# Router logits moved from slot 4 to slot 6, the steps behind them to the next period, and gate scores stored apart from rows

## The chip, the cores and the metric

The kernel runs on one core of one Trainium2 chip. The metric is the device time of the whole program in microseconds, the median of several runs. The profiler records one more execution; its own time stands beside the median below. PE is TensorE, DVE VectorE, ACT ScalarE, POOL GpSimd and SP SyncE; the last is used here to issue DMAs.

## What is computed

The reference is one transformer layer over 8 sequences of 384 tokens of width 512: 256 tokens that a state-space kernel makes from `x`, and 128 of `txt`. Grouped-query attention with rotary embedding follows, then a mixture of 64 experts (top 6 of each token, 64 places for each expert) beside a shared expert. What the change touches is the router:

```python
h = jnp.concatenate([_L0_tok_ref(x, ...), txt], axis=1)
h = h + _L0_attn_ref(_layernorm(h), Wq, Wk, Wv, Wo)
h = h + _L0_ffn_ref(_layernorm(h), gate_w, ...)
# in _L0_ffn_ref
logits = x @ gate_w.T
scores = jax.nn.softmax(logits, axis=-1)
topk_w, topk_i = jax.lax.top_k(scores, K)
...
pos = jnp.zeros((TK,), jnp.int32).at[order].set(pos_sorted)   # place within the expert
valid = pos < CAP
```

## The kernel before

The program has three phases: the state-space kernel (to about 135 us), attention with routing and the first two sequences of the shared expert (to about 924 us), and the experts (to the end). The change lies in the second, `attention_phase`.

**Periods and slots.** Every engine has a queue of its own, whose order is written out by hand. All of them run `for b in ITERATIONS` (b from -1 to 7), and in it 16 slots `n`, one for each of the 16 attention heads. I call an iteration with number b period b. A steady period takes about 78.7 us; period 1 runs from about 271 us, period 3 from 428 us, period 6 from 663 us, period 7 from 737 us. Five sequences are in work at once: a = b+1 is normalised, projected and turned (slots 0 to 7), and its raw scores and row maxima are made (slots 8 to 15); b has its attention (`scores`, `exponentials`, `values`); c = b-1 has its output projection (slots 9 to 15); d = b-2 is routed; e = b-3 has its table entries scattered. The flags `nxt`, `prev2` and `prev3` say whether a, d and e exist. The last period, 7, has no a.

**The routing steps of sequence d, before.** PE turns the normalised rows in slots 2 and 3 (`turn_x2`, L978) and makes the logits in slot 4 (`logits`, L985) in PSUM bank 7. ACT copies them to `at_lg` (L1145). DVE takes maxima and their indices (`routing` step 4, L1405 to L1411), the one-hot tables and `at_mask` (step 5, slot 5, L1414 to L1423). ACT makes the exponentials of the gate (L1152, slot 5). PE makes the places from the mask with a triangular matrix (`places`, L996, slot 6, bank 7). DVE scales the gate scores into columns 512 to 575 of the row buffer (step 6, slot 6, L1426 to L1428) and makes positions from places (L1434 to L1436, slot 6; `at_lg` is used again as `over`). POOL adds the first place of each expert and multiplies with the one-hot table (`places` on POOL, L1597 to L1603, slot 7). One period later DVE sums to slot numbers (`slots`, L1441 to L1445, slot 1), and POOL scatters them with 18 indirect DMAs (L1616, from slot 8). SP stores rows and scores together (`store_rows`, L781).

**Beside it, for sequence a.** `project_q` and `project_kv` (L874) on PE in slots 1 to 5, `rope` on DVE (L1338 to L1340) one slot behind each, the sum of its two halves on POOL (`rope_sum`, L1588, slots 3, 4 and 6), the copy of v on ACT (L1209, slots 3, 4 and 6), and in slot 7 `turn_heads` (L953) on PE, with ACT's copies (`qhi` L1230, bf16 L1129 and L1133) and DVE's remainders (`q_lo`, L1346). From slot 8 on each raw score (`raw`, L916) waits for the row maximum (`row_maximum`, L1355) of the one two before it, since two PSUM banks are used in turn, and the first waits for the last `q_lo`. DVE's `statistics(a + 1)` (L1305) in slot 4 waits for the rows of the next sequence from DRAM. POOL also makes `out_lo` (L1592, slots 0, 1 and 5), released by ACT's `out_hi` (L1186).

## Time and profile before

| | us |
|---|---|
| median of 3 runs (lowest to highest) | 1470.17 (1469.13 to 1474.4) |
| the profiled execution, its own time | 1472.85 |
| its span, first to last instruction | 1471.1 |
| busy: PE, DVE, ACT, POOL | 1248.9, 757.1, 419.8, 498.9 |
| mean granted TensorE clock | 0.943 |

The page's busy numbers are sums over three phases with different limits; the timelines of single engines tell where in a period an engine stands and who released it. In a timeline row stand the start, the duration of a merged group, engine and line, what it writes and reads, and in brackets the idle time before it with the work that ended that idle time. An entry "x8" is a group of 8 instructions.

### The profile page before, as it was taken

How to read it: one execution, taken by the hardware profiler on the slowest of the kernel's cores; microseconds unless marked ns; L12 is line 12 of the kernel's file. 1: busy time of each engine (PE TensorE's matmuls, PEld its weight loads, DVE VectorE, ACT ScalarE, POOL GpSimd, SP SyncE). 2: the span in 40 equal slices, each digit the busy share in tenths (PEclk: the TensorE clock that was granted, in tenths of full speed). 3: DMA queues.
4: the chain of work that ended last, by engine and by line, in shares of the span. 5: the costliest groups of instructions: out<-in, count | busy, mean ns of one | idle time of the engine just before them, and what ended most of it. 6: DMA issues, size and time to landing. Idle time of an engine off the chain costs nothing. (4 is left out here: it accounts for less than half of the span.)

```text
span 1471.1 us, 23499 instructions
## 1 busy us (share of the span) xinstructions
PE 1248.9 (85%) x9192; PEld 795.6 (54%) x9192; DVE 757.1 (51%) x1667; ACT 419.8 (29%) x695; POOL 498.9 (34%) x453
## 2 busy tenths in 40 slices
PE   5263778889898999999987879999999999969995
PEld 5252443445454454646444868666666666646662
DVE  7993566666776867786854352232233222312321
ACT  2221214444444443535354421111111111111110
POOL 0000101111213434343466374334444434343444
PEclk9597779999999999999999899999999999989998
DMA  3033231312425151524271484799999999888993
GB/s 113 1 75 85 53 72 42 84 42 71 122 60 133 36 136 22 151 42 127 45 230 43 133 277 61 221 312 298 309 327 343 302 329 349 264 259 298 332 284 41
DMA packets 141109, 239.82 MB, mean 163 GB/s; under 512 B 61368, under 2 KB 81480, under 8 KB 141000
## 3 DMA queue, kind: packets, MB, share of 16 engines
q1 hardware_dynamic: 117160, 214.10, 45.8%
q0 software_dynamic: 23840, 24.23, 9.2%
q8 instruction: 73, 1.20, 0.3%
q14 instruction: 36, 0.29, 0.1%
HBM read 175.59 MB, written 38.90 MB: 146 GB/s over the span
## 5 line engine op out<-in xcount | busy, mean ns | idle before, releaser
L1993 POOL DMA_INDIRECT out_rows<-mo_y,mo_scatter_half x128 | 180.9, 1413 | 253.9 <-DMA out_rows<-mo_y,mo_scatter_half 183.7
L1355 DVE TENSOR_REDUCE at_maxes<-at_ps 128x1 f32<-128x384 f32 x384 | 195.3, 552 | 63.3 <-PE at_ps L916 56.6
L1122 ACT ACTIVATE bulk<-at_ps 128x1152 f32<-128x1152 f32 x128 | 144.6, 1129 | 272.2 <-PE at_ps L883 250.5
L1616 POOL DMA_INDIRECT slot_table<-at_toki,at_si x144 | 143.6, 997 | 105.7 <-DVE at_maxes L1355 74.0
L70 PE MATMUL mo_ps<-arena_view,arena_view 128*117 128x384 f32 (+1 forms) x864 | 168.8, 344 | 1.1 <-PEq L570 1.1
L70 PEld LDWEIGHTS mo_ps<-arena_view,arena_view 128*117 128x117 f32 (+1 forms) x864 | 146.5, 179 | 14.6 <-issue 14.5
L916 PE MATMUL at_ps<-late_view,late_view 128*128 128x384 bf16 x384 | 117.0, 355 | 35.9 <-DVE at_maxes L1355 18.1
L874 PE MATMUL at_ps<-arena_view,arena_view 128*128 128x512 f32 (+1 forms) x576 | 115.6, 352 | 3.8 <-ACT arena_view L1209 2.3
L874 PEld LDWEIGHTS at_ps<-arena_view,arena_view 128*128 128x128 f32 x576 | 90.7, 193 | 36.9 <-issue 22.4
L916 PEld LDWEIGHTS at_ps<-late_view,late_view 128*128 128x128 bf16 x384 | 31.2, 98 | 145.4 <-DVE at_maxes L1355 108.5
L883 PE MATMUL at_ps<-arena_view 97*128 97x384 f32 x384 | 97.8, 364 | 9.6 <-DMA arena_view<-at_mrow 5.1
L1968 DVE SCALAR_TENSOR_TENSOR mo_hm<-mo_sil,mo_wcol,mo_ps 128x352 f32<-128x352 f32 x32 | 18.6, 581 | 157.2 <-ACT mo_sil L1892 140.6
L874 PE MATMUL at_ps<-late_view,late_view 128*128 128x512 f32 x288 | 92.9, 438 | 6.2 <-DVE at_hr L1388 3.4
L1588 POOL TENSOR_TENSOR arena_view<-arena_view,arena_view 128x640 f32<-128x640 f32 x24 | 37.3, 1556 | 173.5 <-DVE arena_view L1340 173.4
L1592 POOL TENSOR_TENSOR late_view<-arena_view,late_view 128x384 fp32r<-128x384 f32 x32 | 32.2, 1016 | 178.4 <-ACT late_view L1186 178.3
L1838 PE MATMUL mo_ps<-late_view,mo_xgT 128*64 128x352 f32 x512 | 80.6, 468 | 12.5 <-DVE mo_xgT L1961 12.5
L902 PE MATMUL at_ps<-bulk,at_ones 128*32 128x384 f32 x768 | 87.9, 528 | 1.8 <-issue 1.4
L78 PE MATMUL mo_ps<-arena_view,arena_view 117*128 117x512 f32 (+1 forms) x324 | 78.9, 397 | 4.8 <-DVE arena_view L1925 4.8
L883 PEld LDWEIGHTS at_ps<-arena_view 97*128 97x128 f32 x384 | 68.5, 195 | 26.2 <-ACT bulk L1122 8.3
L902 PE MATMUL at_ps<-bulk,arena_view 128*32 128x384 f32 x768 | 82.6, 504 | 0.0
L1838 PE MATMUL mo_ps<-bulk,mo_xgT 128*64 128x352 f32 x512 | 79.3, 462 | 0.2 <-DVE mo_xgT L1961 0.2
L78 PEld LDWEIGHTS mo_ps<-arena_view,arena_view 117*128 117x128 f32 (+1 forms) x324 | 59.6, 188 | 20.9 <-ACT arena_view L1880 5.5
...
## 6 DMA issues: line engine op xcount, KB each, us to landing
...
```

The source lines that it names most:

```text
L70: m = T.matmul(out, self.gu[:, wa, g, k, self.SO[c]:self.SO[c] + self.SW[c]], self.x2[:, xa, k, :], start=(n == 0), stop=(n == last))
L78: m = T.matmul(out, self.h[0:self.SW[c], xa, c, s * P:(s + 1) * P], self.d[0:self.SW[c], wa, c, :], start=(n == 0), stop=(n == last))
L874: m = T.matmul(out, xs[:, xa, k, x_cols], ws[:, wa, k, w_cols], start=(n == 0), stop=(n == 3 * KC - 1))
L883: m = T.matmul(ps[:, kt, 0:SEQ], QT[:, NH + h // REP, kt * P:(kt + 1) * P], QT[:, h, :], start=True, stop=True)
L902: m = T.matmul(ps[HD * j:HD * (j + 1), 3 + sums, 0:SEQ], w, PT[:, (REP * G + j) % RING, kt, :], start=(kt == 0), stop=(kt == NT - 1))
L916: T.matmul(ps[:, raw_bank(a, u), 0:SEQ], qb[:, r, s * P:(s + 1) * P], kb[:, g, :], start=True, stop=True).then_inc(raw_scores, 1)
L1122: A.activation(PT[:, N % RING, :, :], ps[:, 0:NT, 0:SEQ], ACT.Exp, scale=float(HD) ** -0.5)\
L1355: V.tensor_reduce(maxes[:, half, s, h:h + 1], ps[:, raw_bank(a, u), 0:SEQ], AX.X, ALU.max, negate=True)\
L1588: G.tensor_tensor(r1[:, s], r1[:, s], r2[:, s % 2], ALU.add).then_inc(rope_add, 1)
L1616: G.indirect_dma_start(slot_table, bass.IndirectOffsetOnAxis(ap=si[:, e % 2, m:m + 1], axis=0), toki[:, e % 2, m // TOPK:m // TOPK + 1], N ...
L1838: m = M.matmul(ps[CAP * e:CAP * (e + 1), 1 + g, 0:I], xgT[:, k, CAP * e:CAP * (e + 1)], wgu[j][:, e, g, k, :], start=(k == 0), stop=(k == ...
L1993: G.indirect_dma_start(acc_halves, bass.IndirectOffsetOnAxis(ap=scatter_half[:, half, 2 * p + e:2 * p + e + 1], axis=0), y[:, p % 2, e, co ...
```

## The change

The logits move from slot 4 to slot 6 (in periods with a next sequence), and everything behind them goes to the next period, so that a sequence is routed as e and not as d: maxima and indices (step 4) to slot 1, one-hot tables and mask (step 5) to slot 2, exponentials to slot 2 on ACT, PE's places to slot 4, gate scores (step 6) to slot 3, positions (now step 7 of its own) to slot 4, POOL's places to slot 5, `slots` on DVE to slot 7 (it was slot 1). The scatter stays in slots 8 to 15 of the same period. In period 7 the sequence e is finished in slots 0 to 5 and d is routed in slots 4 to 9 as before; the scatters of e start at slot 4 and not 2. Rows are stored as soon as they are normalised, the gate scores by a DMA of their own (`store_scores`), 384 pieces of 64 words for each sequence, with a semaphore `scores_stored` that DVE's step 6, SP and POOL wait for. Who waits for bank 7 changes with it: `turn_heads` and `project_out` wait for the logits' copy and not for the positions.

```diff
+        ROUTE_SLOT = {2: (5,), 3: (6,), 4: (7,)}
+        LAST_ROUTE_SLOT = {0: (4, 5), 1: (6,), 3: (7,)}
...
             def store_rows(d):
+                sp.wait_ge(x2_ready, NT * (d + 1))
+                sp.dma_start(xrow[d * SEQ:(d + 1) * SEQ, 0:D].rearrange("(s p) d -> p s d", p=P),
+                             x2_of(d)[:, :, 0:D]).then_inc(x2_stored, 16)
+
+            def store_scores(d):
                 sp.wait_ge(score_rows, d + 1)
-                sp.dma_start(xrow[d * SEQ:(d + 1) * SEQ, :].rearrange("(s p) d -> p s d", p=P), x2_of(d))\
-                    .then_inc(x2_stored, 16)
+                sp.dma_start(xrow[d * SEQ:(d + 1) * SEQ, D:D + E].rearrange("(s p) d -> p s d", p=P),
+                             x2_of(d)[:, :, D:D + E]).then_inc(scores_stored, 16)
...
                 if i == 2:
-                    wait(pe, pos_read, a - 2)
+                    wait(pe, lg_copied, a - 2)
...
                     for q in steps[0:1]:
                         values(G, q)
-                    if prev2 and n == 4:
+                    if prev3 and n == (4 if nxt else 2):
+                        places(e)
+                    if prev2 and n == (6 if nxt else 4):
                         logits(d)
-                    if prev2 and n == 6:
+                    if prev2 and not nxt and n == 6:
                         places(d)
...
-                    if prev2 and n == 5:
+                    if prev3 and n == (2 if nxt else 1):
+                        gate_exponentials(e)
+                    if prev2 and not nxt and n == 5:
                         gate_exponentials(d)
...
                     dve.wait_ge(gexp_ready, NT * (d + 1))
+                    wait(dve, scores_stored, 16 * d)
...
-                if n == 6:
+                if n == 7:
                     dve.wait_ge(pos_ready, d + 1)
...
-                    if prev3 and n == 1:
-                        slots(e)
+                    if prev3 and nxt and n == 1:
+                        routing(e, 4)
...
-                    if prev2:
-                        routing(d, n)
+                    if prev3:
+                        for step in (ROUTE_SLOT if nxt else LAST_ROUTE_SLOT).get(n, ()):
+                            routing(e, step)
+                    if prev3 and n == (7 if nxt else 4):
+                        slots(e)
...
-                    if prev2 and n == 7:
+                    if prev3 and n == (5 if nxt else 3):
+                        places(e)
+                    if prev2 and not nxt and n == 7:
                         places(d)
...
-                    if b == B - 1 and 2 <= n < 8:
-                        scatter(e, 3 * (n - 2), 3 * (n - 1))
+                    if b == B - 1 and 4 <= n < 10:
+                        scatter(e, 3 * (n - 4), 3 * (n - 3))
```

Three places in the engines' queues, first of the kernel before, then of the changed one. Line numbers of the changed kernel are up to 43 higher.

**POOL, slots 3 to 7 of a steady period.** The first row holds the rope sums of slots 3 and 4, the next two the inverse deviation, the fourth `out_lo`; `at_slot`, `at_lg` and `at_hv` mark the places. Before:

```order
L1588 TENSOR_TENSOR arena_view_1739<-arena_view_1739,arena_view_1740 128x640 x2
L1581 TENSOR_TENSOR at_rstd<-at_ve,at_mhalf 128x3
L1583 TENSOR_TENSOR at_shift<-at_shift,at_rstd 128x3
L1592 TENSOR_TENSOR late_view_1738<-arena_view_1748,late_view_1738 128x384
L1588 TENSOR_TENSOR arena_view_1739<-arena_view_1739,arena_view_1740 128x640
L1597 TENSOR_TENSOR late_view_1750<-late_view_1750,at_slot 128x192
L1599 TENSOR_TENSOR late_view_1750<-late_view_1750,at_lg 128x192
L1603 TENSOR_TENSOR at_hv<-at_hot,late_view_1750 128x384 x3
```

and in the changed kernel:

```order
L1631 TENSOR_TENSOR arena_view_1739<-arena_view_1739,arena_view_1740 128x640 x2
L1624 TENSOR_TENSOR at_rstd<-at_ve,at_mhalf 128x3
L1626 TENSOR_TENSOR at_shift<-at_shift,at_rstd 128x3
L1635 TENSOR_TENSOR late_view_1738<-arena_view_1748,late_view_1738 128x384
L1640 TENSOR_TENSOR late_view_1750<-late_view_1750,at_slot 128x192
L1642 TENSOR_TENSOR late_view_1750<-late_view_1750,at_lg 128x192
L1646 TENSOR_TENSOR at_hv<-at_hot,late_view_1750 128x384 x3
L1631 TENSOR_TENSOR arena_view_1739<-arena_view_1739,arena_view_1740 128x640
```

The three rows of places stood behind the last rope sum (slot 6) and now stand ahead of it, behind `out_lo`.

**DVE, from the end of slot 6 to the start of slot 8.** The transposes and the reciprocal are of the softmax sums, the group of five is `q_lo`, `at_maxes` are the row maxima of slot 8. Before:

```order
L1372 STREAM_TRANSPOSE arena_view_1747<-at_ps 128x384
L1373 RECIPROCAL at_rcol<-arena_view_1747 128x12
L1374 STREAM_TRANSPOSE arena_view_1747<-at_rcol 128x384
L1346 TENSOR_TENSOR arena_view_1742<-at_ps,arena_view_1741 128x384 x5
L1355 TENSOR_REDUCE at_maxes<-at_ps 128x1 x2
```

and in the changed kernel:

```order
L1405 STREAM_TRANSPOSE arena_view_1747<-at_ps 128x384
L1406 RECIPROCAL at_rcol<-arena_view_1747 128x12
L1407 STREAM_TRANSPOSE arena_view_1747<-at_rcol 128x384
L1379 TENSOR_TENSOR arena_view_1742<-at_ps,arena_view_1741 128x384 x5
L1476 TENSOR_REDUCE at_sf<-at_hv 128x18
L1478 CAST at_si<-at_sf 128x18
L1479 CAST at_toki<-at_tokf 128x3
L1480 TENSOR_SCALAR at_tokf<-at_tokf 128x3
L1388 TENSOR_REDUCE at_maxes<-at_ps 128x1 x2
```

The four rows of `slots` (`at_sf`, `at_si`, `at_toki`, `at_tokf`) stood in slot 1 and now stand between the last `q_lo` and the first row maximum.

**PE, slot 4 to the start of slot 7.** `gwT` marks the logits, `at_upper` the places, 128x512 and 128x256 are the projections of q and kv, `bulk` the values, 128x384 of `arena_view` alone the scores of a head; the last row is the first turn of the heads. Before:

```order
L985 MATMUL at_ps<-gwT,at_x2T 128x64 x12
L902 MATMUL at_ps<-bulk,at_ones 32x384 x4
L874 MATMUL at_ps<-arena_view_65,arena_view_1737 128x512 x12
L883 MATMUL at_ps<-arena_view_1746 128x384 x3
L902 MATMUL at_ps<-bulk,at_ones 32x384 x4
L902 MATMUL at_ps<-bulk,arena_view_1745 32x384 x4
L874 MATMUL at_ps<-arena_view_65,arena_view_1737 128x256 x12
L883 MATMUL at_ps<-arena_view_1746 128x384 x3
L902 MATMUL at_ps<-bulk,arena_view_1745 32x384 x4
L996 MATMUL at_ps<-at_mask,at_upper 128x64 x9
L883 MATMUL at_ps<-arena_view_1746 128x384 x3
L953 MATMUL at_ps<-late_view_54,arena_view_1739 128x128 x9
```

and in the changed kernel:

```order
L1025 MATMUL at_ps<-at_mask,at_upper 128x64 x9
L922 MATMUL at_ps<-bulk,at_ones 32x384 x4
L894 MATMUL at_ps<-arena_view_65,arena_view_1737 128x512 x12
L903 MATMUL at_ps<-arena_view_1746 128x384 x3
L922 MATMUL at_ps<-bulk,at_ones 32x384 x4
L922 MATMUL at_ps<-bulk,arena_view_1745 32x384 x4
L894 MATMUL at_ps<-arena_view_65,arena_view_1737 128x256 x12
L903 MATMUL at_ps<-arena_view_1746 128x384 x3
L922 MATMUL at_ps<-bulk,arena_view_1745 32x384 x4
L1008 MATMUL at_ps<-gwT,at_x2T 128x64 x12
L903 MATMUL at_ps<-arena_view_1746 128x384 x3
L973 MATMUL at_ps<-late_view_54,arena_view_1739 128x128 x9
```

Logits and places have changed their positions; PE's work up to the turn of the heads is the same.

## Rows read from the trace of the kernel before

**Rows 1.** Page, part 1: busy us (share of the span) of each engine
```profile
PE 1248.9 (85%) x9192; PEld 795.6 (54%) x9192; DVE 757.1 (51%) x1667; ACT 419.8 (29%) x695; POOL 498.9 (34%) x453
```

**Rows 2.** PE's waits, 190 to 860 us: total us, times, longest
```profile
PE at_ps L916 <- DVE at_maxes L1355: 15.2, 28, 1.6
...
PE at_ps L996 <- DVE at_mask L1423: 7.5, 6, 3.1
```

**Rows 3.** PE timeline, period 3, slots 4 to 8: start, us, group [idle <-releaser]
```profile
446.87 2.89 PE L985 MATMUL at_ps<-gwT,at_x2T 128*128 128x64 f32 x24
...
459.26 0.43 PE L996 MATMUL at_ps<-at_mask,at_upper 128*128 128x64 bf16 x9 [0.90 <-DVE at_mask L1423]
459.54 0.77 PE L883 MATMUL at_ps<-arena_view 97*128 97x384 f32 x3
461.45 0.84 PE L953 MATMUL at_ps<-late_view,arena_view 128*128 128x128 f32 x6 [1.15 <-POOL arena_view L1588]
...
467.47 0.80 PE L916 MATMUL at_ps<-late_view,late_view 128*128 128x384 bf16 x2 [0.99 <-issue]
...
469.64 0.82 PE L916 MATMUL at_ps<-late_view,late_view 128*128 128x384 bf16 x2
```

**Rows 4.** PE timeline, period 1, slots 7 and 8
```profile
302.39 0.79 PE L883 MATMUL at_ps<-arena_view 97*128 97x384 f32 x3 [0.50 <-ACT bulk L1122]
...
309.74 0.49 PE L916 MATMUL at_ps<-late_view,late_view 128*128 128x384 bf16 x2 [2.70 <-issue]
```

**Rows 5.** POOL timeline, period 3, slots 4 to 7
```profile
452.93 1.56 POOL L1588 TENSOR_TENSOR arena_view<-arena_view,arena_view 128x640 f32<-128x640 f32 x1 [11.64 <-DVE arena_view L1340]
...
455.73 1.03 POOL L1592 TENSOR_TENSOR late_view<-arena_view,late_view 128x384 fp32r<-128x384 f32 x1
459.81 1.54 POOL L1588 TENSOR_TENSOR arena_view<-arena_view,arena_view 128x640 f32<-128x640 f32 x1 [3.06 <-DVE arena_view L1340]
462.56 0.59 POOL L1597 TENSOR_TENSOR late_view<-late_view,at_slot 128x192 f32<-128x192 f32 x1 [1.21 <-DVE at_lg L1435]
...
463.91 2.68 POOL L1603 TENSOR_TENSOR at_hv<-at_hot,late_view 128x384 f32<-128x384 bf16 x3
```

**Rows 6.** POOL timeline, period 6, slots 5 and 6
```profile
690.79 1.02 POOL L1592 TENSOR_TENSOR late_view<-arena_view,late_view 128x384 fp32r<-128x384 f32 x1 [8.14 <-ACT late_view L1186]
693.92 1.55 POOL L1588 TENSOR_TENSOR arena_view<-arena_view,arena_view 128x640 f32<-128x640 f32 x1 [2.11 <-DVE arena_view L1340]
```

**Rows 7.** DVE timeline, period 3, slots 1 to 8
```profile
433.45 1.34 DVE L1441 TENSOR_REDUCE at_sf<-at_hv 128x18 f32<-128x1152 f32 x1
434.83 0.93 DVE L1443 CAST at_si<-at_sf 128x18 uint32<-128x18 f32 x1
...
436.27 0.69 DVE L1338 TENSOR_TENSOR arena_view<-at_ps,at_cos 128x512 f32<-128x512 f32 x1 [0.24 <-DVE at_tokf L1445]
...
449.82 1.88 DVE L1305 BATCH_NORM_STATS2 at_bn<-arena_view 128x6 f32<-128x512 f32 x3 [5.71 <-DMA arena_view<-in_txt]
...
467.98 1.02 DVE L1355 TENSOR_REDUCE at_maxes<-at_ps 128x1 f32<-128x384 f32 x2 [0.62 <-PE at_ps L916]
```

**Rows 8.** DVE timeline, period 7, slot 9
```profile
776.88 0.25 DVE L1443 CAST at_si<-at_sf 128x18 uint32<-128x18 f32 x1
```

**Rows 9.** ACT timeline, period 3, slot 5
```profile
455.55 0.34 ACT L1152 ACTIVATE late_view<-at_lg,at_nm 128x64 f32<-128x64 f32 x1
```

**Rows 10.** PE timeline, period 3, slot 3
```profile
443.64 1.66 PE L874 MATMUL at_ps<-arena_view,arena_view 128*128 128x256 f32 x12 [0.15 <-ACT arena_view L1209]
```

**Rows 11.** PE timeline, period 6, slot 8
```profile
701.58 0.49 PE L916 MATMUL at_ps<-late_view,late_view 128*128 128x384 bf16 x2 [0.99 <-issue]
...
702.78 0.58 PE L916 MATMUL at_ps<-late_view,late_view 128*128 128x384 bf16 x2
```

**Rows 12.** Busy time by 1 us stretches; the third number from the end is PEclk
```profile
468.00:469.00 1.00, 1.00 (x9) 0.20 (x8) 1.00 (x3) 0.12 (x1) 0.00 (x0) 0.50 0.53 109
```

**Rows 13.** PE timeline, period 7, slot 2
```profile
745.23 0.55 PE L978 MATMUL at_ps<-late_view,late_view 128*128 128x128 f32 x3 [2.26 <-ACT late_view L1163]
```

40 lines of the change are left out of this document (34 added, 6 removed).

## The prediction

> **What bounds the kernel now.** I read the page's busy shares first: PE is busy 85% of the span, DVE 51%, POOL 34%, ACT 29% [rows 1], so a change outside PE pays only where PE waits. Then PE's waits over the attention phase: raw scores wait for the row maxima in slots 8 to 15 (15.2 us in 28 waits), which the change doesn't remove, and the places wait for the mask (7.5 us in 6 waits) [rows 2]. The biggest of those six, 3.1 us, lies after the last period, where the order stays. Last, the timelines of a steady period, to see what comes behind each wait.
>
> In period 3, PE waits 0.90 us for the mask in slot 6 and 1.15 us for the last rope sum before the heads are turned; from the scores of head 7 (459.54) to the first raw score (467.47) it takes 7.93 us [rows 3]. Period 1 has no routing at all: the same stretch, 302.39 to 309.74, still takes 7.35 us [rows 4]. So the floor under slot 7 isn't routing: it is exponentials, `qhi`, bf16 copies and `q_lo` in ACT's and DVE's queues. Of all that routing costs there, only 7.93 - 7.35 = 0.58 us and the 0.90 us of the mask can come back, 1.48 us a period, whatever waits vanish from the list.
>
> **What the change does in periods 2 to 6.** PE's work up to the turn of the heads is the same: 2.89 us of logits go behind the projections, and the places (0.43 us) come ahead [rows 3].
>
> (1) Period 2 routes its d and has no e, so it only loses steps: no mask, no positions, no `slots`. It becomes a period 1 with logits in slot 6. Gain 0.90 + 0.58 = 1.48 us, and some 0.2 us for the places that it no longer makes: **-1.7**.
>
> (2) ACT now makes three gate exponentials of 0.34 us [rows 9], about 1.1 us with their short reads, in slot 2, ahead of the exponentials of head 3 and the copy of v. PE waits for this copy already (0.15 us [rows 10]), so it stands in a chain without slack: the projection of k and v in slot 3 starts about 0.9 us later in periods 3 to 6. Alone this would cut the gain to 0.6 us.
>
> (3) POOL decides the turn of the heads. In slot 5 it makes `out_lo` (1.03 us from 455.73) and then nothing until the last rope sum at 459.81 [rows 5]. The changed queue puts the places between these two. They take 0.59 + 0.59 + 2.68 us and two gaps of 0.08, from 462.56 to 463.91 + 2.68 = 466.59: 4.03 us [rows 5]. They can't start sooner: the rope sum of slot 4 starts at 452.93, released by DVE's rope behind the statistics, which wait 5.71 us for DRAM until 449.82 [rows 5, 7], and this DMA is issued early in the period by SP, in the old order. POOL is then occupied without a break: `out_lo` to 456.76, places to about 460.85, rope sum to about 462.4. Before it ended at 461.35. PE arrives at 459.54 - 0.90 + 0.9 + 0.77, about 460.4, and waits until 462.5, against 461.45 before [rows 3]: instead of a gain of 0.6 a loss of 1.05 us. In period 6, without statistics, ACT releases `out_lo` at 690.79; with PE 2.89 - 0.43 - 0.9 = 1.5 us ahead in slot 5 (logits gone, places come, (2) against it) it starts near 689.4, places end near 694.5, and the rope sum starts there and not at 693.92 [rows 6]: +0.6. Periods 4 and 5 lie between +0.25 and +0.5 by the same sum, for their `out_lo` starts earlier on POOL than in period 3. Together **+2.4**. Bounds: 0.58 saved in each period if POOL had no queue (-2.3), and 4.03 less the idle 3.06 us ahead of the rope sum [rows 5] plus 0.6 for contention, +1.6 in each (+6.4). I take the value of the timeline, since each of its pieces has a row. The wait for `at_lg` (it holds POOL's operand) delays ACT's copy of the logits to the same 461, ahead of the turn; it decides nothing.
>
> (4) `slots` leaves slot 1, where DVE waited 0.24 us before the next rope in any case (433.45 to 436.03, then 436.27 [rows 7]); PE doesn't wait there, and steps 4 to 6 fit into slots 1 to 3 ahead of the 5.71 us wait. I cost that at nothing. In slot 7 it stands where nothing covers it: between the last `q_lo`, which releases the first raw score, and the first row maximum, which releases the third. It is 1.34 us of sum, a cast and small ones. The cast takes 0.93 us in slot 1 beside `out_lo` on POOL and 0.25 us in period 7 [rows 7, 8]; in slot 7 POOL is free, so 1.9 us in all and 0.2 us to the next instruction. A maximum is 0.5 us (two in 1.02 [rows 7]). The third raw score can start 2.6 us after the first. Before it started 469.64 - 467.47 = 2.17 us after it in period 3 [rows 3] and 702.78 - 701.58 = 1.20 us in period 6 [rows 11]. The difference between these two is the clock: in period 3 the granted clock is 0.50 there, which is 1.2 GHz [rows 12], and the first pair of raw scores takes 0.80 us against 0.49 [rows 3, 11]. So the new wait is 0.45 us in the slow periods (3 and 4) and 1.4 us in the others (5 and 6). In the slow ones I add 0.35 us, for the next three raw scores find the maxima late as well. **+4.4** in four periods. Bounds: +1.8 (0.45 each) and +8.4 (the whole 2.1 us).
>
> The Trainium skill ("SBUF — State Buffer", section "SBUF: two separate sides") says that DVE and GpSimd share a port pair as an exclusive lock, held for a whole instruction. The two casts agree with it. If the lock met `slots` in slot 7 too, the term would be 0.7 us larger in each period, by the rows' 0.93 and 0.25.
>
> (5) Period 7 gets steps 4 and 5 of e on DVE and its exponentials ahead of `normalised2(d)` on ACT. PE waits already 2.26 us for that normalisation [rows 13]; 1.1 us more stand ahead of it, and the places of e in slot 2 wait for the mask about as long: +1.35. Against it, POOL's places of d in slot 7 have 9 scatters ahead of them and no longer 18, and DVE waited for them in slot 9: -0.35. **+1.0**, bounds 0 and +3.
>
> (6) Stores: SP issues one more DMA for each sequence. In steady periods rows and scores leave between the loads of the period and the stack of slot 7, where SP's queue waits anyway; behind the last period the wait for the scores stands where the wait for rows and scores stood. POOL's scatters start from slot 8 as before. Nothing.
>
> **Sum.** -1.7 + 2.4 + 4.4 + 1.0 = +6.1 us. Against the profiled execution's own 1472.85 that is 1478.95. It stood 2.7 us above the median of the three runs, so I forecast 1470.17 + 6.1 = **1476.3 us**, 0.4% slower. The experts phase hangs on the end of this one, so all of it counts.
>
> **The rivals.**
> - *The waits go and nothing takes their place.* PE gains the whole 1.48 us in five periods: 1470.2 - 7.4 = 1462.8. For it speaks that both named waits vanish. Against it stand POOL's queue and the maxima. It decides from the point at which POOL's places end before the rope sum's operands are there, and DVE's `slots` meets a PE that waits anyway. On the other side of no change than my forecast: 12%.
> - *Only `slots` costs.* POOL gets to the places sooner than I have it (`out_lo` first of all), and the last rope sum isn't held: -1.7 - 4 x 0.6 + 4.4 + 1.0 = +1.3, 1471.5. For it speaks that in period 6 the margin is only 0.6 us: 20%.
> - *The clock falls further.* The idle time of PE is gathered into two gaps of 2 us around the turn of the heads instead of five of about 1 us. Rows show the granted clock at 0.50 after such a stretch in period 3 [rows 12] and not in period 6. If periods 5 and 6 fall too and 3 and 4 stay low longer, 1.2 us each (0.31 us for each pair of raw scores [rows 3, 11], about four such groups with the values between them): 1476.3 + 4.8 = 1481: 20%.
> - *My forecast*, 1472 to 1480: 48%.
>
> **How the numbers follow.** A measurement of this kernel can tell about 0.5% (7.4 us) from no change: below 1462.8 faster, above 1477.5 slower. The first rival is half below the line: faster 0.07. The clock case and about a third of my own lie above: slower 0.36. The rest is 0.57. The range of 8 in 10 leaves out most of the first rival and the outer half of the clock case: 1465 to 1484.
>
> **What would show it.** In the changed kernel's periods 3 to 5: the mask wait of PE gone; POOL's three places rows straight behind `out_lo` and the rope sum straight behind them with no idle time; PE's turn of the heads waiting some 2 us for L1631; `slots` between `q_lo` and the first maximum; the third raw score 2.6 us after the first; a wait of about 1 us in slot 3 for the copy of v. Periods 3 to 6 should be longer by 1.4 to 2 us, period 2 shorter by 1.7. I am wrong if the turn of the heads comes earlier in the period than before, or if the periods are as long as before although the rows stand so.

## The result

The changed kernel takes 1487.24 us (median of 4 runs, 1484.58 to 1491.80) beside 1472.29 us for the kernel before (4 runs, 1469.13 to 1475.32): a ratio of 1.0117, 95% interval 1.0079 to 1.0155 (the two medians alone differ by 15.0 us, 1.0%). I had forecast 1476.3 with a range to 1484: slower, as forecast, but by more than twice as much, and outside the range. Run again on another chip (e5 below) the changed kernel stood at 1.0094 (1.0053 to 1.0134), 13.8 us by that run's median of before, 1467.92. The times of one kernel on one chip differ by more than the change does (12 executions of the changed kernel in e5: 1470.96 to 1493.42), so I compare stretches of traces below, and ratios within one chip.

The profiled execution took 1484.58 us (span 1482.8). Part 1 of its page, answering [rows 1], says little: nearly the same shares, as many instructions, 8 us more PE time.

```profile
PE 1256.8 (85%) x9192; PEld 801.3 (54%) x9192; DVE 751.3 (51%) x1667; ACT 417.9 (28%) x695; POOL 503.5 (34%) x453
```

PE's waits between 190 and 870 us (total, times, longest), answering [rows 2]:

```profile
PE at_ps L936 <- DVE at_maxes L1388: 19.5, 34, 1.6
PE at_ps L936 <- issue: 18.0, 7, 2.7
PE at_ps L1025 <- DVE at_mask L1456: 7.0, 3, 3.6
...
PE at_ps L894 <- ACT arena_view L1240: 5.6, 8, 0.9
PE at_ps L973 <- issue: 5.3, 4, 1.7
...
PE at_ps L922 <- DVE arena_view L1405: 4.2, 1, 4.2
```

The mask's six waits have become three, in period 7 and behind it. In their place stand 34 waits for maxima where there were 28, the copy of v (0.9 us), the turn of the heads and, once, 4.2 us for L1405 (the inverted sums), a wait that the kernel before doesn't have. The timeline of PE in period 3, slots 3 to 8, answering [rows 3] and [rows 10]:

```profile
446.32 1.67 PE L894 MATMUL at_ps<-arena_view,arena_view 128*128 128x256 f32 x12 [0.92 <-ACT arena_view L1240]
...
458.53 2.89 PE L1008 MATMUL at_ps<-gwT,at_x2T 128*128 128x64 f32 x24
...
463.61 2.14 PE L973 MATMUL at_ps<-late_view,arena_view 128*128 128x128 f32 x9 [1.62 <-issue]
...
470.24 0.61 PE L936 MATMUL at_ps<-late_view,late_view 128*128 128x384 bf16 x2 [1.72 <-issue]
...
472.71 0.97 PE L936 MATMUL at_ps<-late_view,late_view 128*128 128x384 bf16 x2 [0.42 <-DVE at_maxes L1388]
```

The logits are in slot 6 (458.53), no places and no mask stand there; the projection in slot 3 waits 0.92 us; the turn of the heads (L973) waits 1.62; the third raw score starts 2.47 us behind the first. POOL and DVE in the same period, answering [rows 5] and [rows 7]:

```profile
457.03 1.02 POOL L1635 TENSOR_TENSOR late_view<-arena_view,late_view 128x384 fp32r<-128x384 f32 x1
458.01 0.59 POOL L1640 TENSOR_TENSOR late_view<-late_view,at_slot 128x192 f32<-128x192 f32 x1
458.68 0.59 POOL L1642 TENSOR_TENSOR late_view<-late_view,at_lg 128x192 f32<-128x192 f32 x1
459.35 2.67 POOL L1646 TENSOR_TENSOR at_hv<-at_hot,late_view 128x384 f32<-128x384 bf16 x3
461.98 1.53 POOL L1631 TENSOR_TENSOR arena_view<-arena_view,arena_view 128x640 f32<-128x640 f32 x1
```

```profile
469.11 1.02 DVE L1379 TENSOR_TENSOR arena_view<-at_ps,arena_view 128x384 fp32r<-128x384 f32 x2 [0.37 <-ACT arena_view L1261]
470.05 1.34 DVE L1476 TENSOR_REDUCE at_sf<-at_hv 128x18 f32<-128x1152 f32 x1
...
472.09 1.02 DVE L1388 TENSOR_REDUCE at_maxes<-at_ps 128x1 f32<-128x384 f32 x2 [0.21 <-DVE at_tokf L1480]
```

POOL runs through from `out_lo` over the places to the rope sum, which ends at 463.5, where PE starts; DVE makes `slots` (470.05 to 471.9) between the last `q_lo` and the first maximum. Step for step it stands as the prediction drew it, but for `out_lo`, which starts 0.7 us earlier in the period (29.2 us behind the first turn of x, not 29.9). What it had not drawn is in the clock. Busy time of PE in stretches of 4 us around the first raw scores of period 4 (the last numbers are the granted clock, the DMA share and GB/s), first of the kernel before, then of the changed one, starting 3.2 to 3.4 us ahead of the first of them:

```profile
542.98:546.98 4.00, 3.19 (x15) 0.50 0.17 63
546.98:550.98 4.00, 4.00 (x24) 0.74 0.82 167
550.98:554.98 4.00, 3.89 (x28) 1.00 0.81 173
```

```profile
547.46:551.46 4.00, 1.28 (x10) 1.00 0.00 0
551.46:555.46 4.00, 2.80 (x18) 0.62 0.83 172
555.46:559.46 4.00, 4.00 (x20) 0.53 0.87 178
559.46:563.46 4.00, 4.00 (x27) 1.00 0.09 20
```

Before, the clock is at 0.50 (1.2 GHz, the lower of its two levels) while PE turns heads and waits for ACT and DVE in any case, and is back at 1.00 some 2.7 us behind the first raw score (546.37). Now PE idles for 2.7 us ahead of the first raw score (1.28 of 4 us busy, clock 1.00), and the clock falls behind that, for some 6 us, over raw scores and values that bound the period.

### The profile page after: what moved, and what is told of

It reads as the page before. It is cut to its first block and busy times, and to the rows that moved or that the text cites. A ratio compares the mean times of both kernels' runs of the same rounds, so it can differ in the third digit from the quotient of the medians.

```text
span 1482.8 us, 23520 instructions
## 1 busy us (share of the span) xinstructions
PE 1256.8 (85%) x9192; PEld 801.3 (54%) x9192; DVE 751.3 (51%) x1667; ACT 417.9 (28%) x695; POOL 503.5 (34%) x453
## 5 line engine op out<-in xcount | busy, mean ns | idle before, releaser
L2039 POOL DMA_INDIRECT out_rows<-mo_y,mo_scatter_half x128 | 185.3, 1447 | 241.8 <-DMA out_rows<-mo_y,mo_scatter_half 155.0
L936 PE MATMUL at_ps<-late_view,late_view 128*128 128x384 bf16 x384 | 120.7, 367 | 47.2 <-DVE at_maxes L1388 21.8
L903 PE MATMUL at_ps<-arena_view 97*128 97x384 f32 x384 | 100.9, 373 | 11.6 <-ACT bulk L1153 6.5
```

Source lines behind the costliest of these rows:

```text
L903: m = T.matmul(ps[:, kt, 0:SEQ], QT[:, NH + h // REP, kt * P:(kt + 1) * P], QT[:, h, :], start=True, stop=True)
L936: T.matmul(ps[:, raw_bank(a, u), 0:SEQ], qb[:, r, s * P:(s + 1) * P], kb[:, g, :], start=True, stop=True).then_inc(raw_scores, 1)
L2039: G.indirect_dma_start(acc_halves, bass.IndirectOffsetOnAxis(ap=scatter_half[:, half, 2 * p + e:2 * p + e + 1], axis=0), y[:, p % 2, e, co ...
```

## Where the time is

I cut each trace at three kinds of rows: the first turn of x of each period (L946, L926 before), the first turn of x2 in period 7, and the places of sequence 6 behind the last period. All in us; "remote" is the idle time of ACT and DVE that the profile puts down to a cause of that name, over the whole run. It is in all kernels of three of the five sessions and in none of the other two, so it isn't a kernel's own; where it is present the last stretch can't be compared. The profiled execution of e7, 1491.37 us, is the longest of its ten; its excess lies in the last stretch and behind it.

```
kernel                         P2     P3     P4     P5   P6 to   x2 of 7    remote
                                                         x2 of 7 to places
before                        78.84  78.70  78.74  77.62  84.30   90.66      28.7
changed                       76.98  81.22  81.03  80.27  89.28   93.27      44.4
e5 changed, again             77.09  79.12  79.86  80.40  89.31   93.19      13.9
e2 store first                77.77  79.86  80.34  81.86  89.57   86.89       0
e1 slots ahead                77.73  79.67  80.19  78.31  88.24   88.09       0
e3 pool behind                77.07  81.63  81.72  81.99  90.68   89.06       0
e4 before + dummy slots       77.34  79.71  78.58  78.86  85.48   84.06       0
e6 slots ahead, store first   77.70  79.70  80.23  80.07  87.39  102.17      47.3
e7 changed + fillers          76.77  79.03  79.05  79.05  87.62  102.92      40.8
e8 before + fillers           77.71  77.39  77.41  77.45  83.97   91.37      18.4
e9 slots ahead + fillers      76.74  78.24  78.32  78.17  86.79   89.11       0
e10 and pool behind + fillers 76.70  79.67  79.44  78.03  87.00   88.32       0
e11 period 7                  77.70  79.87  80.29  80.17  88.64   83.74       0
e12 all                       76.08  80.70  78.74  78.79  85.54   82.37       0
e13 mid                       76.41  76.74  75.83  75.78  85.15   89.35      46.8
e14 mid, exponentials early   76.13  76.60  76.60  76.60  85.92   86.39      12.0
e15 mid, no filler            77.04  78.33  77.04  77.61  87.45   87.73      12.5
e16 mid, pool ahead           76.78  78.98  78.21  77.74  86.13   84.91      12.7
```

The changed order of periods 2 to 6 was traced four times (changed, e5, e2 and e11, whose edits lie in period 7). The means of the first three against the one trace of before: period 2 -1.6, periods 3 to 5 +6.3 (241.3 against 235.1), period 6 to the turn of x2 +5.1. For the last stretch I take kernels without "remote": e1, e3, e9 and e10 have the changed end, 88.6 on average, e4 that of before, 84.06: +4.6. Sum +14.4 us (14.0 with e11), against 13.8 by the ratio of e5.

This sum is put together from several traces, and it is softer than its digits. In the first pair of traces the last stretch is only 2.6 us longer (93.27 against 90.66), both with "remote", and periods 2 to 7 together 13.2. The changed trace is also 3.8 us late at the start of period 2, ahead of the change, and takes 5.3 us less behind the places of sequence 6 (629.9 against 635.2), a part in which all the traces here lie between 620.8 and 642.3 us. So a time of a single execution says nothing on the change. e3, e4, e9, e10, e14 and e16 were executed once each (1479.40, 1468.54, 1472.40, 1472.38, 1469.11 and 1450.86 us): of these only the stretches can be used. And one trace of before is a narrow base. Period 2 of e4 is the kernel before without any edit, and it took 77.34 us where before has 78.84. In both PE idles 1.15 us ahead of the turn of the heads and 1.00 ahead of the first raw score; behind that score the clock was at 0.57 in before and at 1.00 in e4. The 4 us from it on, before and then e4:

```profile
388.61:392.61 4.00, 4.00 (x21) 0.57 0.72 147
```

```profile
390.02:394.02 4.00, 3.94 (x27) 1.00 0.71 147
```

## The experiments

**e1: slots ahead of q_lo.**

```diff
+                    if prev3 and nxt and n == 7:
+                        slots(e)
                     if nxt and n == 7:
                         for i in range(NTILE):
                             q_lo(a, i)
...
-                    if prev3 and n == (7 if nxt else 4):
+                    if prev3 and not nxt and n == 4:
```

> The changed kernel with one move: slots(e) of the steady periods stands ahead of the five q_lo of slot 7 on VectorE and no longer between them and the first row maxima. There VectorE is idle (5.1 us of waiting for ScalarE in period 4). Length of a period is taken from one turn of x to the next: 81.22, 81.03 and 80.27 us for periods 3 to 5 in the changed kernel, 78.70, 78.75 and 77.62 in the kernel before. If slots costs its own delay alone (the wait of 1.20 us ahead of the third raw score), the periods shorten by 1.2 us each, the granted clock staying at 0.50 over slot 8. If slots is the whole loss, its gap also being what brings the clock down over slot 8, they shorten by 2.3 to 2.6 us each, to 78.5 to 78.9. If it is POOL's queue that costs, by less than 0.5 us.

Ratio to before 1.0012 (0.9975 to 1.0050), against 1.0094 to 1.0117 with `slots` where the change has it. The wait ahead of the third raw score is gone: the first and the third in period 3 of e1,

```profile
468.02 0.78 PE L936 MATMUL at_ps<-late_view,late_view 128*128 128x384 bf16 x2 [1.81 <-issue]
...
470.17 0.82 PE L936 MATMUL at_ps<-late_view,late_view 128*128 128x384 bf16 x2
```

2.15 us apart at half clock, as before. Periods 3 to 5 sum to 238.2, 3.1 less than the mean of the changed order, with a spread from 78.3 to 80.2: in period 5, the short one, the clock is back at 1.00 before the first raw score, in the other two it is at 0.50 behind it. The ratio would make `slots` most of the loss, but with period 6 the stretches give back 4.3 us and no more, and e6, with this edit and another, stands at 1.0049 on another chip. The periods are about 1 us shorter each: between "POOL's queue" and the lower of the two figures that I had set for `slots`, and something else varies.

**e2: the store ahead of the loads.**

```diff
+                if prev3 and not nxt:
+                    store_scores(e)
                 if b == B - 1:
                     load_shared_weights()
-                if prev3 and not nxt:
-                    store_scores(e)
```

> The changed kernel with one move: in period 7 SyncE issues the store of the scores of e ahead of the loads of the shared weights and no longer behind them. In the changed kernel VectorE waits 5.02 us for this store at 775.5 to 780.6, ahead of the scores of d, and TensorE 4.24 us behind it for the inverted sums (783.32). If this store is the loss of period 7, both waits vanish and the tail starts 3.5 to 4.5 us earlier against the start of period 7. If the wait only stands in the place of the 3.4 us that the kernel before waits there for its residual, that one returns and less than 1 us is won. A third way: SyncE now waits for the score rows (ready at 760) before it issues the weights, so that ScalarE's pieces of the weights come 5 us later and the wait turns up there.

Ratio 1.0062 (1.0024 to 1.0100). In the changed kernel DVE stood still in period 7 ahead of the scores of d, since it may not overwrite those of e before they are stored, and `divide`'s inverted sums stand behind it. DVE and PE there:

```profile
780.56 0.18 DVE L1460 RECIPROCAL at_rsum<-at_ssum 128x3 f32<-128x3 f32 x1 [5.02 <-DMA rows_scores<-late_view]
...
782.59 0.58 DVE L1405 STREAM_TRANSPOSE arena_view<-at_ps 128x384 f32<-128x384 f32 x1 [0.22 <-issue]
```

```profile
783.32 1.51 PE L922 MATMUL at_ps<-bulk,at_ones 128*32 128x384 f32 x8 [4.24 <-DVE arena_view L1405]
```

SP issued that store at 768.11, behind the loads of the shared weights (766.59 and 767.02); its 96 KB landed 12 us later. In e2 it is issued at 762.03 ahead of them, neither wait is there, the two stores of this size land 3.4 and 7.8 us after their issue, and no wait for the weights shows. The last stretch takes 86.89 us and not 88.6 (88.1 to 89.1 in four traces), so by this one trace the wait was worth about 1.7 us of its 4.2: the rest is covered by PE's next waits (3.72 us for a residual, 5.53 for `out_lo`).

**e3: POOL's places behind the rope sum.**

```diff
-                    if prev3 and n == (5 if nxt else 3):
+                    if prev3 and not nxt and n == 3:
                         places(e)
...
                         rope_sum(a, KV_SLOT[n - 1])
+                    if prev3 and nxt and n == 6:
+                        places(e)
```

> The changed kernel with one move: GpSimd makes the places of e behind the last rope sum of slot 6 and no longer ahead of it. In period 3 out_lo ends at 458.0, so the sum would run at 458.0 to 459.6 and TensorE, which has its scores done at 461.99, would turn the heads 1.5 us earlier, at about 462.1 instead of 463.61 (33.4 us behind the turn of x; 33.2 in the kernel before). If POOL's queue costs what I forecast, periods 3 to 5 shorten by about 1.5 us each, those of period 3 most. If the time between turn and first raw score is bound elsewhere, the turn comes earlier and the period keeps its length to 0.5 us, the slow stretch of the clock then lying otherwise. Slots has its operand by 463.6 and is not delayed.

Counted from the first turn of x of the period, as all times with a plus below, the turn of the heads comes at +34.0 us in all periods, 1.6 to 1.9 earlier in periods 3 to 5, and these are on average the longest of all, 81.6 to 82.0. Neither of the two ways that I had set out. ACT, period 4:

```profile
541.20 0.33 ACT L1176 ACTIVATE at_lg<-at_ps 128x192 f32<-128x192 f32 x1 [4.86 <-POOL at_hv L1646]
...
542.44 0.88 ACT L1261 ACTIVATE arena_view<-at_ps 128x384 fp32r<-128x384 f32 x2
```

The copy of the logits (`at_lg`) waits 4.86 us for POOL's last product, because `over` lies in `lg`'s buffer, and the exponentials of head 7 and `qhi` stand behind it in ACT's queue. The first raw score is then on average 1 us later than without the move (0.4, 1.3 and 1.2 us in periods 3 to 5). So POOL's places hold `qhi` on two paths: over the last rope sum and the turn of the heads, and over the copy of the logits and the exponentials. In period 4 of the changed kernel the second ends at 544.56, and ACT then waits 0.68 us for the turned heads, which come last. The move makes the first path shorter, but behind the rope sum POOL's last product ends 2.1 us later in the period (+36.1, not +34.0), and the second path, longer by as much, takes over.

**e4: a dummy slots in the kernel before.**

```diff
                             q_lo(a, i)
+                        if prev3:
+                            link(V.tensor_reduce(sf[:], iota[:, :].rearrange("p (a e) -> p a e", a=1)
+                                                 .to_broadcast([P, NT * TOPK, E]), AX.X, ALU.add), route_step)
+                            link(V.tensor_copy(sf[:], sf[:]), route_step)
+                            link(V.tensor_scalar(sf[:], sf[:], 1.0, None, ALU.add), route_step)
```

> The kernel before with one addition: behind the q_lo of slot 7, from period 3 on, VectorE makes a reduction of the size of slots (18 x 64 elements, a constant table as input), a copy and an addition of 18 elements. No value that is used changes. By my forecast for slots the third raw score of periods 3 and 4 starts 2.5 us behind the first, 0.3 us later than before, period 6 1.3 us later, and each period is longer by that, 0.5 to 1.4 us. If the gap brings the granted clock down over slot 8 as well, periods 3 to 5 are longer by 1.5 to 2.5 us. With no effect, slots is out as a cause.

Its third raw score stands 2.23 us behind the first in every period. Where the clock was up there before (period 5, period 6), the stretch is 1.24 and 1.18 us longer: the forecast term. Period 3 is 1.0 longer, period 4 0.2 shorter, with the clock at 1.00 in all of slots 7 and 8 of that period, where it had been at 0.50 in the kernel before. Together +3.3 us in these four, forecast 0.5 to 1.4 each. That fits the forecast of `slots`, but it is one trace, and period 2, where nothing was added, came out 1.5 us shorter than in before: whether and where the clock falls is worth as much as the gap, and this run can't tell the two apart in a period.

**e5: the changed kernel again.** No edit.

> The changed kernel itself, unedited, on the chip of the next three and beside the kernel before. In the first measurement it stood at a ratio of 1.0117; its profile held 26 us of ScalarE waits of a kind ('remote') that none of the four experiments so far shows, the kernel before 19 us. If these belong to the chip or the execution and not to the change, the ratio falls to what the periods show: 5.6 us over periods 2 to 5 and 4 to 5 us over periods 6 and 7, 1.006 to 1.008. If they belong to the change, it stays at 1.011 to 1.012. Periods 2 to 5 together 319.2 to 320.1 us either way (319.5 and, in the kernel with the store moved, 319.8).

Ratio 1.0094 (1.0053 to 1.0134): between the two figures. The order is slower on this chip too. The interval overlaps that of the first result (1.0079 to 1.0155), so whether a part of that one went with the "remote" waits (44.4 us in that profile, 28.7 in before's, 13.9 here) is not shown. Periods 2 to 5 took 316.5 us and not 319.2 to 320.1: the same kernel differs by 3 us from trace to trace there, with the stretches of half clock lying otherwise.

**e6: slots ahead and the store first.** The edits of e1 and e2.

> The changed kernel with both moves, slots ahead of q_lo in the steady periods and the store of scores ahead of the loads of the shared weights in period 7. Slots alone stood at 1.0012 of the kernel before, the store alone at 1.0062. If the two losses are apart, the ratio is 1.0012 less the store's 1 to 3 us, 0.999 to 1.001, periods 2 to 5 as in slots alone (315.9 us, 2.0 over the kernel before), and the waits of 4.60 us (VectorE for the store) and 4.40 (TensorE for the sums) gone. A ratio under 0.998 would say that the change, put so, pays.

Ratio 1.0049 (1.0016 to 1.0081), above the 0.999 to 1.001 that I expected, and I can't say why: its trace has 47 us of "remote", 12.9 us in one residual of the last stretch. Periods 3 to 5 are at 240.0, P6 at 87.4. It doesn't contradict e1 in the stretches, and adds nothing on the end.

**e7 and e8: fillers.** Matmuls of constants keep PE at work in its waits from period 1 on; the counts in e7 are 16, 24 and 14, in e8 14, 6 and 0.

```diff
+            def filler(bank, count):
+                for _ in range(count):
+                    T.matmul(ps[:, bank, 0:P], upper[:, 0, :], upper[:, 1, :], start=True, stop=True)
...
+                    if prev and nxt and n == 8:
+                        wait(pe, divide_step, DIVIDE_STEPS * (G - 1) + 1)
+                        filler(4, 24)
                     for u in units[0:2]:
                         raw(of, u)
...
+                    if prev and nxt and n == 7:
+                        pe.wait_ge(rope_q, NT * (a + 1))
+                        filler(5, 16)
                     if nxt and n == 7:
                         turn_heads(a, 0)
...
+                    if prev and nxt and n == 8:
+                        filler(7, 14)
                     for u in units[2:4]:
                         raw(of, u)
```

> The changed kernel with TensorE kept at work in its waits of slots 7 and 8 from period 2 on: 16 matmuls of constants (bf16, 128 x 128) ahead of the turn of the heads, 24 ahead of the first raw score and 14 ahead of the third, into banks that hold nothing then. No value that is used changes. If the granted clock falls to 0.50 over slot 8 because TensorE idled in slot 7, it stays at 1.00 there, and periods 3 to 5 shorten by 1.5 to 2.5 us each, to 78.5 to 79.5, though the 1.20 us of wait ahead of the third raw score stay (now filled). If the clock falls by a rule that has nothing to do with this idle time, the stretch at 0.50 stays and the fillers only lie in waits or push: the periods keep their length or grow by up to 0.7 us.

> The kernel before with the same fillers, shorter: 14 matmuls ahead of the turn of the heads and 6 ahead of the first raw score. Its clock is at 0.50 from the turn to the first raw scores in periods 3 to 5, where TensorE waits in any case. If the idle time brings the clock down, it stays at 1.00 and the periods shorten by 0.3 to 1.0 us each, which is all that the slow stretch costs there, against the 1.5 to 2.5 us in the changed kernel. That would show the same loss of clock to be cheap in the one place and dear in the other. If the clock has another cause, no change or up to 0.5 us longer.

In both the granted clock is 1.00 throughout slots 7 to 9 of periods 3 to 5, and the periods become constant: 79.03, 79.05, 79.05 against 77.39, 77.41, 77.45. PE in period 4 of e7, the filler rows (L1061) with the turn and raw scores, and the clock:

```profile
532.70 1.07 PE L1061 MATMUL at_ps<-at_upper 128*128 128x128 bf16 x16
534.38 1.17 PE L973 MATMUL at_ps<-late_view,arena_view 128*128 128x128 f32 x9 [0.62 <-issue]
...
537.53 1.52 PE L1061 MATMUL at_ps<-at_upper 128*128 128x128 bf16 x24
540.40 0.48 PE L936 MATMUL at_ps<-late_view,late_view 128*128 128x384 bf16 x2 [1.36 <-issue]
```

```profile
540.00:544.00 4.00, 3.15 (x34) 1.00 0.59 123
```

The fillers delay nothing in e7: behind them PE still idles 0.6 us ahead of the turn, 1.36 ahead of the first raw score and 0.32 ahead of the third. That is the cleanest measurement here: at full clock the change costs 1.6 us in each of periods 3 to 5 and 3.65 us from period 6 to the turn of x2. The same stretches without fillers lie on average 1.4 us (changed) and 0.9 to 1.0 us (before) above that in a period, and 1.8 and 0.3 in the last: the rest of the loss of these stretches is clock. With PE's idle time filled the clock doesn't fall, so this idle time brings it down, though not each time (period 2 of before and of e4), and in the changed kernel the low stretch falls on work. The Trainium skill ("TensorE: Matmul & The Clock Gate", Part 1) says that a monitor of how busy PE has been sets the clock to one of two levels; these runs agree. The kernel before pays for the clock too. In its period 5, where the clock is back at 1.00 a microsecond ahead of the first raw score, it takes 0.2 us more than with fillers; in periods 3 and 4, where it is at 0.50 over the first raw scores, 1.3 us more each. As whole kernels, e7 stands at 1.0058 (1.0014 to 1.0103), below the 1.0094 of the changed kernel on that chip, but the intervals overlap. e8 stands at 1.0017 (0.9981 to 1.0053), no better than before, though its periods 3 to 5 are 2.8 us shorter. Where this went I can't say; 18 us of "remote" lie in its trace, and its interval is 11 us wide.

**e9: slots ahead, with fillers.** The edits of e1 and e7.

> The changed kernel with the fillers of before (TensorE's waits filled with matmuls of constants, so that the granted clock stays at 1.00) and slots ahead of q_lo. With fillers alone every period from 3 to 5 took 79.03 to 79.05 us, with the third raw score 2.47 us behind the first; the kernel before with fillers took 77.39 to 77.45, with 1.20. If slots costs just the difference of these two waits, 1.27 us, the periods take 77.8 us. If slots also held something else, down to 77.4; if the wait moves to another place, it stays above 78.5.

78.17 to 78.32 us. The third raw score now stands 1.99 us behind the first and no longer 1.20, since nobody waits there and the 14 fillers stand in the way: 0.79 us of my own making. Taking these off I get 77.4 to 77.5, the 77.4 of e8; no run has this order without those 14. So by this estimate `slots` is the whole loss of a steady period at full clock, 1.6 us, 1.27 of it ahead of the third raw score, and places and early exponentials together cost nothing against before: they use up what the vanished mask wait had given.

**e10: also POOL's places behind, and `over` in its own place.**

```diff
-        over = lg[:]
...
+        over = nc.alloc_sbuf_tensor_at("at_over", [P, NT, E], F32, offset=start + 1152)[:]
...
             def logits_copied(d, bank=7):
                 wait(act, mask_ready, d)
-                wait(act, slot_rows_ready, d)
...
             def gate_exponentials(d):
                 wait(act, score_rows, d)
+                wait(act, slot_rows_ready, d)
```

> As the last one, and GpSimd's places behind the last rope sum. In the third experiment that move alone brought the turn of the heads 1.65 us forward and the period got no shorter, since ScalarE waited 4.86 us for GpSimd's last product before it copied the logits: the place table 'over' lies in the buffer of the logits. Here 'over' has a place of its own (inside the buffer of the products, behind the place of threes), and the copy of the logits waits for nothing of GpSimd's. If the two waits on GpSimd (rope sum behind places, copy of the logits behind places) are all that it costs, the turn comes at +34.0 and the first raw score at +40.0 from the turn of x, and the periods take 76.1 to 76.4 us, 1.5 less than with slots alone and 1.1 less than the kernel before with fillers. If the first raw score is bound otherwise (bf16 copies, q_lo), they stay at 77.4 to 77.8.

Missed: 79.67, 79.44, 78.03. The copy of the logits is free (538.28, released by PE), but `slots`, ahead of the first `q_lo`, now waits for POOL. DVE and PE in period 4:

```profile
540.83 1.35 DVE L1488 TENSOR_REDUCE at_sf<-at_hv 128x18 f32<-128x1152 f32 x1 [4.40 <-POOL at_hv L1660]
...
542.81 1.49 DVE L1391 TENSOR_TENSOR arena_view<-at_ps,arena_view 128x384 fp32r<-128x384 f32 x3
```

```profile
540.65 0.85 PE L922 MATMUL at_ps<-bulk,arena_view 128*32 128x384 f32 x8
543.42 1.54 PE L973 MATMUL at_ps<-late_view,arena_view 128*128 128x128 f32 x6 [1.92 <-DVE arena_view L1391]
```

A third path from the same places, and with PE idle for 1.92 us in a spot that I had not filled the clock fell again in periods 3 and 4.

**e11: period 7.** The store of e2, and fewer scatters inside the period.

```diff
-        SCATTERED_LAST = 10
+        SCATTERED_LAST = 6
...
-            scatter(B - 3, SCATTERED_LAST, SCATTERS)
+            scatter(B - 3, SCATTERED_LAST, 14)
             inverse_deviation2(B - 1)
+            scatter(B - 3, 14, SCATTERS)
```

> The changed kernel, no fillers, with two moves at the end: the store of scores ahead of the loads of the shared weights (as in the second experiment), and only 6 scatters of d in slots 10 to 12 and not 10, the other 12 behind out_lo (8) and behind the last inverse deviation (4). In the second experiment GpSimd's scatters ran without a break to 807.83 + 0.97 = 808.8, and TensorE waited 5.53 us for the out_lo behind them; in the kernel before they ended 2.7 us before out_lo was due and TensorE waited 2.55. If that queue is what is left of the loss in period 7, the wait falls to 2.5 to 2.9 us and the stretch from the first turn of x2 of period 7 to the places of sequence 6 falls from 86.9 to about 84 us (84.1 in the undisturbed kernel before). If the scatters only fall due later, the wait turns up at those places (the mask) or at GpSimd's places, and the stretch stays at 87.

Ratio 1.0051 (1.0022 to 1.0081); the last stretch falls to 83.74 us, that of the kernel before being 84.06. The rows behind it are POOL's last scatter in the period with the three `out_lo` straight behind it and the last `out_lo`, in e2, then PE in e2 and in e11:

```profile
807.83 0.97 POOL L1659 DMA_INDIRECT slot_table<-at_toki,at_si  x1 [0.30 <-issue]
808.82 2.95 POOL L1635 TENSOR_TENSOR late_view<-arena_view,late_view 128x384 fp32r<-128x384 f32 x3
...
815.62 0.99 POOL L1635 TENSOR_TENSOR late_view<-arena_view,late_view 128x384 fp32r<-128x384 f32 x1 [2.75 <-ACT late_view L1217]
```

```profile
816.76 0.77 PE L894 MATMUL at_ps<-late_view,late_view 128*128 128x512 f32 x1 [5.53 <-POOL late_view L1635]
```

```profile
813.17 1.16 PE L894 MATMUL at_ps<-late_view,late_view 128*128 128x512 f32 x4 [3.17 <-POOL late_view L1635]
```

Between the two POOL makes the inverse deviation (to 812.9), for which ACT waits 6.54 us with the normalisation and the last `out_hi`; so the chain runs from the scatters over POOL, ACT and POOL again to PE. A scatter mostly costs POOL 0.97 us and 0.30 of gap, 28 of them about 36 us by that, and since `slots(e)` moved from slot 1 to slot 4 of period 7 they start later and end only where PE's last values end (808.80 and 808.93 in e2). The wait of 5.5 (6.76 in e1) falls to 3.2; it was 2.55 in the kernel before. With store and scatters moved the last stretch is back at the length of before, 83.74 against 84.06, one trace each: together they are its loss in the traces without "remote". In the first trace of the changed kernel "remote" held PE and ACT longer than the scatters held POOL, which waited 4.20 us for ACT ahead of `out_lo`: there they were covered.

**e12: all together.** Edits of e1, e2, e10 and e11, gate exponentials in slot 3 behind the copy of v (`n == (3 if nxt else 1)`), fillers 16, 24 and 0.

> All together: slots ahead of q_lo, 'over' in its own place and GpSimd's places behind the rope sum, the gate exponentials behind the copy of v in slot 3, the store and the scatters of period 7 as in the last one, and the fillers ahead of the turn and ahead of the first raw score. Periods 3 to 5 at 75.3 to 76.3 us, as in the last but one and up to 0.9 less if the copy of v comes 0.9 us earlier and nothing takes its place, against 77.6 to 78.8 in the kernel before. That is 2.5 us in each of five periods and 1 us at the end: a ratio of 0.990 to 0.993 to the kernel before. If the moves don't add up, 0.996 to 1.000.

Ratio 1.0001 (0.9971 to 1.0030): the changed order brought back to the time of before, no more; I had expected 0.990 to 0.993. DVE again waits 4.40 us for POOL ahead of `slots`, the first raw score comes at +42.7 to +44.5, and the 24 fillers, at half clock, take 2.78 us and not 1.52.

**e13 to e16: slots between the second and the third q_lo.**

```diff
                         for i in range(NTILE):
                             q_lo(a, i)
+                            if prev3 and i == 1:
+                                slots(e)
```

e13 is e12 with this, without the filler ahead of the turn; e14 is e13 with the exponentials back in slot 2; e15 is e13 without fillers; e16 is e13 with POOL's places ahead, `over` in `lg` and the exponentials in slot 2, as the change has them.

> As e12_all, with slots between the second and the third q_lo and no longer ahead of the first, and no filler ahead of the turn of the heads (TensorE doesn't wait there now). In e12_all VectorE waited 4.40 us for GpSimd's last product before slots, so the first q_lo came 3.1 us late, TensorE idled 2.60 us between the second and third group of turned heads, and the granted clock fell to 0.50. Between q_lo 1 and 2 VectorE idles 1.8 us for ScalarE in the changed kernel (546.85 to 548.64), and slots takes 1.9. If that gap holds it, the first raw score comes at +40.0 to 40.4 from the turn of x, the third 1.20 behind it, and periods 3 to 5 take 75.8 to 76.3 us at a clock of 1.00: 1.2 to 1.6 less than the kernel before with fillers, 2.4 to 2.9 less than without. Ratio 0.990 to 0.994. If the places of GpSimd come too late for slots in this place too, 77 to 79 us.

> e13_mid with the gate exponentials where the change puts them, in slot 2 ahead of the exponentials of head 3 and the copy of v. By my step (2) the projection in slot 3 then waits 0.9 us for the copy of v. If this delay reaches the turn of the heads now that nothing of GpSimd's stands there, the turn and the whole period are 0.5 to 0.9 us later than in e13_mid. If the wait of VectorE for the rows of the next sequence absorbs it, they are the same to 0.2 us.

> e13_mid without fillers: what remains is the clock. TensorE still idles some 2.7 us between its last scores of slot 7 and the first raw score. If this gap is what brings the clock down over slot 8, periods 3 to 5 are longer than in e13_mid by 1 to 2 us and differ among each other by up to 1 us; if the gap alone is not enough, now that there is no wait ahead of the turn, the clock stays at 1.00 and they are as long as in e13_mid.

> The changed kernel with slots between the second and the third q_lo, the two moves of period 7 and the filler ahead of the first raw score, but GpSimd's places ahead of the last rope sum, 'over' in the buffer of the logits and the gate exponentials in slot 2, as the change has them. Against the kernel before with fillers (77.4) only my steps (2) and (3) are left in periods 3 to 5. By my sum they cost 0.25 to 1.05 us: 77.7 to 78.5. If slots was the whole loss of a period at full clock, 77.3 to 77.6.

e13: ratio 0.9933 (0.9900 to 0.9967), 1457.38 us beside 1465.95, as I had expected. It is faster than the kernel before, and the interval stays under 1. Periods 4 and 5 take 75.8 us, period 3 76.7. DVE and PE, period 4:

```profile
534.50 1.02 DVE L1391 TENSOR_TENSOR arena_view<-at_ps,arena_view 128x384 fp32r<-128x384 f32 x2 [3.23 <-ACT arena_view L1273]
535.60 1.35 DVE L1488 TENSOR_REDUCE at_sf<-at_hv 128x18 f32<-128x1152 f32 x1
...
537.59 1.66 DVE L1391 TENSOR_TENSOR arena_view<-at_ps,arena_view 128x384 fp32r<-128x384 f32 x3
```

```profile
532.62 1.15 PE L973 MATMUL at_ps<-late_view,arena_view 128*128 128x128 f32 x9
...
536.49 1.52 PE L1061 MATMUL at_ps<-at_upper 128*128 128x128 bf16 x24
539.35 0.49 PE L936 MATMUL at_ps<-late_view,late_view 128*128 128x384 bf16 x2 [1.34 <-issue]
...
540.55 0.57 PE L936 MATMUL at_ps<-late_view,late_view 128*128 128x384 bf16 x2
```

`slots` lies in DVE's idle time, the turn stands at +33.3 without a wait, the third raw score 1.20 us behind the first, the clock is 1.00. e14 has 76.60 in all three periods: the early exponentials cost 0.8 us a period as soon as nothing of POOL's hides them (period 3 of e13 is no shorter; its turn comes 0.9 us later than in periods 4 and 5, for PE waits 0.93 us in slot 5 for the copy of v, behind DVE, whose statistics wait 2.00 us for DRAM there and 1.06 in period 4). e15 has 78.33, 77.04, 77.61 and a ratio of 1.0032 (1.0001 to 1.0063): the fillers alone are worth 1.5 us a period here, and they decide between faster than before and not: the two intervals lie apart. In the kernel before fillers were worth 0.9 us a period and no better ratio (e8). Against that trace the periods of e13 are still 0.7 to 1.7 us shorter, which is what its order gives; the two were never timed on one chip. e16 has 78.98, 78.21, 77.74; the last at a full clock, 1.1 us above e14 and 0.3 above the kernel before with fillers, the first two with 2.62 and 2.09 us of idle time ahead of the turn (1.70 in the last) and a clock of 0.50 behind it. Its period 3 lies above the 77.7 to 78.5 that I had set.

## Why the prediction was wrong

The sum had +6.1 us and 14.4 are measured. By its own steps:

- **(1) Period 2**, -1.7: measured -1.6 against the one trace of before, but that is in part luck. That trace has a fall of the clock there, and e4, the same code, has none and took 77.34 us: against it the gain is 0.1. With fillers it is 0.9 (76.77 in e7, 77.71 in e8). A gain is shown, its size isn't.
- **(2) Early exponentials**: the projection in slot 3 waits 0.92 us in periods 3 to 6, forecast 0.9. Right, and by e14 worth 0.8 us a period once other waits are gone.
- **(3) POOL's queue**, +2.4: the rows stand as drawn, the turn of the heads waits 1.4 to 1.7 us in periods 3 to 5. But the turn came only 0.1 to 0.4 us later in the period than before (to 0.5 in e5, 1.2 once in e2), where I had 1.05 in period 3 and 0.6 in period 6: `out_lo` started 0.7 us earlier than I put it (29.2 us behind the turn of x, not 29.9). At full clock (2) and (3) cost nothing net, by the estimate of e9. "It decides nothing" of the logits' copy was true of the change and false of every repair (e3).
- **(4) `slots`**, +4.4: the gap is 2.47 us in all four periods, forecast 2.6; the price at full clock is 1.6 us each by e9, forecast 1.4 (and 0.8 in the slow periods). Here the mechanism was right. By luck the errors of (3) and (4) cancel: the clean periods 3 to 5 give 4.9 us (237.13 - 232.25) where steps (3) and (4) had 4.8.
- **The clock** was no term of the sum but a rival, at 1.2 us in each of four periods and 20%. It is real, and smaller than that: 1.4 us over periods 3 to 5 and 1.4 in period 6 on top of the clean difference. The step that failed is the sentence of (4) that took the clock of the periods as given ("0.45 us in the slow periods (3 and 4) and 1.4 us in the others (5 and 6)"). I had read it as falling on some periods and not on others, when it falls behind idle time of PE, and the idle 2.7 us now sit right ahead of work that bounds the period: period 6, at 1.00 throughout in before, is at 0.50 for some 6 us behind the first raw score in all the traces of the changed order.
- **(5) and (6), period 7**: +1.0 and "nothing". Up to the turn of x2 it was right (places wait 3.60 where the normalisation had 2.26, +1.34; forecast 1.35). Behind it I had -0.35 and measured +4.6 (+2.6 in the first pair of traces, with "remote" in both). I had followed the stores through the steady periods and behind the last one, and not through period 7, where two loads of weights stand between, and I had counted fewer scatters ahead of POOL's places but not that the same 28 scatters now end when `out_lo` is long due. This is the biggest mis-sized term: 4.9 of the 8.3 us missing.

The first measurement stood a little higher than the second (1.0117 and 1.0094); their intervals overlap, and no cause for a difference is shown.

The rivals: "the waits go" and "only `slots` costs" are out as totals, though the second is true of the steady periods at full clock, by the estimate of e9. "The clock falls further" had the right cause at 2.8 of its 4.8 us, and missed period 7 as my own sum did. What would have told in advance: SP's order of issues in period 7, and 28 scatters of 1.27 us laid on POOL's time from slot 4 to `out_lo`. Both were there to be asked for.
